# Moving wavelet and normalisation work between VectorE, GpSimd and ScalarE, and taking the quantiser's range from row extremes of h

## The reference

```python
# 1. wavelet tokeniser: three Haar analysis levels, then per level
w = softmax(stack([h, v, d]).reshape(B, -1) @ Wd + bd)          # 3 weights per image and level
rec = idwt2(rec, h * w[:, 0], v * w[:, 1], d * w[:, 2])         # Haar synthesis
h = rec
# 2. h = h + mixer(layernorm(h)): projections, a softplus, a cumulative sum along the
#    rows of an image, two products with Wc and Wd, biases bc + bd
# 3. h = h + ffn(layernorm(h)), quantised:
scale = sigmoid(clip_x) * max(abs(xn)) / 127                    # xn = layernorm(h), one scale for all
xq    = clip(round(xn / scale), -128, 127) * scale
gate, up = xq @ quant(w_gate).T, xq @ quant(w_up).T             # 704 columns
out   = quant(silu(gate) * up) @ quant(w_down).T
layernorm(x) = (x - mean(x)) / sqrt(var(x) + 1e-5)              # over a row of 256
```

## Time and profile before

| | us |
|---|---|
| median of 3 runs | 154.51 (152.99 to 154.53) |
| the profiled execution | 153.44 |
| its span, first to last instruction | 151.7 |
| VectorE busy in the span | 130.2 (86%) |
| TensorE busy | 116.7 (77%) |
| ScalarE busy | 78.3 (52%) |
| GpSimd busy | 43.7 (29%) |

### The profile page before, as it was taken

One profiled execution on the slowest core, in us unless ns is written; L12 is line 12 of the kernel. 1 busy time (PEld: TensorE's weight loads), 2 busy tenths in 40 slices (PEclk: granted clock), 3 DMA queues, 4 the chain that ended last, 5 costly groups with the idle time before them and its releaser, 6 DMA issues.

```text
span 151.7 us, 1953 instructions
## 1 busy us (share of the span) xinstructions
PE 116.7 (77%) x655; PEld 78.7 (52%) x660; DVE 130.2 (86%) x257; ACT 78.3 (52%) x143; POOL 43.7 (29%) x58
## 2 busy tenths in 40 slices
PE   0659839997779972999999903968999998799710
PEld 0649737896355451864888803334545433475400
DVE  0799599963599999999999999859989898999991
ACT  4004107103296642076398079977999990794000
POOL 6631000000400099950000404000766570005720
PEclk9999955999758999599999995599999999999996
DMA  4999700000000000000000000000000000001176
GB/s 110 385 367 402 327 4 6 0 0 0 0 0 0 0 6 0 0 0 0 0 0 4 0 0 2 0 0 0 2 4 0 0 0 0 0 4 69 73 230 181
DMA packets 3035, 8.26 MB, mean 54 GB/s; under 512 B 466, under 2 KB 722, under 8 KB 2898
## 3 DMA queue, kind: packets, MB, share of 16 engines
q1 hardware_dynamic: 2738, 7.62, 14.1%
q10 hardware_dynamic: 288, 0.52, 0.9%
HBM read 6.05 MB, written 2.10 MB: 54 GB/s over the span
## 4 chain that ended last, share of the span: by engine, by line
DVE 51%; PE 21%; ACT 11%; issue 10%; DMA 3%; POOL 2%; ACTq 0%; DVEq 0%; POOLq 0%
PE bank L471 6%; PE bank L414 4%; PE bank L444 4%; DVE middle L1223 4%; DVE state_mem L1230 3%; DVE stats L987 3%; DVE wabs L1027 3%; DVE amax L1196 3%; DVE raw L1255 3%; PE bank L419 3%; DMA early<-in_x 3%; ACT early L773 3%; DVE early L1005 3%; ACT raw L874 3%; ACT state_mem L867 2%
## 5 line engine op out<-in xcount | busy, mean ns | idle before, releaser
L389 POOL TENSOR_TENSOR rstd<-var,minus_half 128x8 f32<-128x8 f32 x4 | 6.8, 1702 | 61.7 <-DVE var L993 61.7
L614 PE MATMUL bank<-state_mem,wqT 128*128 128x512 bf16 x78 | 18.2, 379 | 0.8 <-DVE state_mem L1186 0.6
L401 POOL TENSOR_TENSOR early<-raw,state_mem 128x512 f32<-128x512 f32 x10 | 13.0, 1298 | 18.3 <-ACT raw L874 18.3
L773 ACT ACTIVATE early<-h,nmr,rstd 128x256 f32<-128x256 f32 x25 | 12.8, 587 | 6.7 <-DVE nmr L998 6.7
L558 PE MATMUL bank<-mixer_w,early 128*128 128x256 f32 x64 | 16.0, 407 | 0.0
L867 ACT ACTIVATE state_mem<-bank,gscale 128x512 f32<-128x512 f32 x22 | 15.1, 752 | 1.2 <-PE bank L614 1.0
L627 PE MATMUL bank<-wqT,middle 128*128 128x256 bf16 (+1 forms) x96 | 12.8, 274 | 2.4 <-DVE middle L1223 2.4
L419 PE MATMUL bank<-restart,ident 128*128 128x512 bf16 x47 | 13.6, 440 | 1.2 <-DVE var L993 0.9
L558 PEld LDWEIGHTS bank<-mixer_w,early 128*128 128x128 f32 x64 | 12.9, 207 | 3.0 <-issue 1.1
L1196 DVE TENSOR_REDUCE amax<-early 128x1 f32<-128x1024 f32 x11 | 13.3, 1212 | 0.4 <-POOL early L401 0.3
L614 PEld LDWEIGHTS bank<-state_mem,wqT 128*128 128x128 bf16 x80 | 7.4, 98 | 10.0 <-DVE early L1204 1.1
(11 more groups left out here) (148 smaller groups left out, 244.8 us busy)
## 6 DMA issues: line engine op xcount, KB each, us to landing
out<-early SPq DMA_DIRECT2D x7, 256.0 KB, 2.8
early<-in_x SPq DMA_DIRECT2D x1, 1024.0 KB, 9.0
wT<-in_dot_weights SPq DMA_DIRECT2D x1, 784.0 KB, 7.0
raw<-in_gate_rows SPq DMA_DIRECT2D x1, 768.0 KB, 10.6
raw<-in_up_rows SPq DMA_DIRECT2D x1, 768.0 KB, 11.9
raw<-in_down_rows SPq DMA_DIRECT2D x1, 768.0 KB, 13.2
early<-in_x ACTq DMA_DIRECT2D x2, 256.0 KB, 4.9
early<-in_x SPq DMA_DIRECT2D x2, 256.0 KB, 4.7
```

Of the source, the lines that this page charges most:

```text
L401: nc.gpsimd.tensor_tensor(act[:, u, :], up_s[:, m % UPS, :], silu[:, u % SIL, :], ALU.mult).then_inc(pool_act_ready, 1)
L614: last = nc.tensor.matmul(dst[:, :], w, xqT[:, k, c, :], start=(c == 0), stop=(c == CH - 1))
L773: nc.scalar.activation(xn[:, half, r, :], h[:, half, r, :], ACT.Identity, bias=nmr[:, norm, half, r:r + 1], scale=rstd[:, norm, half, r:r ...
```

## The change

Five things change.

1. Half 1's wavelet analysis goes to GpSimd (`analyse_second`), except the sums across columns and the two low bands of level 0, which VectorE keeps (`across_second`, `low_second`). TensorE's `haar_level` and ScalarE's copies of it go.
2. In the last synthesis level of both halves ScalarE scales the band D too, and GpSimd forms the two sums of V and D (`high_columns`).
3. The power -0.5 becomes Ln and Exp on ScalarE (`inverse_std`), right behind the moments; ScalarE normalises all rows; `add_bias` goes pair by pair.
4. The largest |xn| comes from the largest and the smallest element of each row of `h` (`extremes`, `reach_from_mean`), times the row's inverse deviation.
5. 32 of the 36 weight transposes stand ahead of most of half 1's mixing on TensorE, and their copies on ScalarE ahead of the second normalisation. `WARM_FFN` goes from 14 to 10. `weight_maxima(0)` moves to the wavelet stage, `coefficients` behind `xn_out(0)`.

```diff
+            def analyse_second():
+                add = nc.gpsimd.tensor_tensor
+                pool.wait_ge(x_in[-1], 16)
+                src = xt[:, 1, :, :]
+                seq.link(add(lohi1[0][:, 1, :, :], src[:, :, 0::2], src[:, :, 1::2], ALU.subtract))
+                for op, b in ((ALU.add, V_), (ALU.subtract, D_)):
+                    add(dst[:, b, :, :], lohi1[0][:, 1, 0::2, :], lohi1[0][:, 1, 1::2, :], op).then_inc(high_bands, 1)
+                pool.wait_ge(low_bands, 1)
+                for n in (1, 2):
...
+            def high_columns(half):
+                pool.wait_ge(v_ready, 4 * half + 4)
+                for odd, op in enumerate((ALU.add, ALU.subtract)):
+                    nc.gpsimd.tensor_tensor(syn[0][:, 1, odd::2, :], v, d, op).then_inc(high_ready, 1)
...
+            def inverse_std(norm, half):
+                sc.wait_ge(stats_ready, norm * HALVES + half + 1)
+                seq.link(nc.scalar.activation(var[...], stats[:, norm, half, :, 2], ACT.Ln, bias=eps[:, :], scale=1.0 / C))
+                nc.scalar.activation(rstd[...], var[...], ACT.Exp, scale=-0.5).then_inc(rstd_ready, 1)
...
             softplus(0)
             decay_rate(0)
-            normalise(0, 1, range(ACT_ROWS[1]))
+            inverse_std(0, 1)
+            normalise(0, 1, range(R))
...
+            def extremes(half, n):
+                nc.vector.tensor_reduce(hmax[:, half, rows], h[:, half, rows, :], AX.X, ALU.max)
+                return seq.mark(nc.vector.tensor_reduce(hmin[:, half, rows], h[:, half, rows, :], AX.X, ALU.min))
...
+            for n in range(R // 2):
+                step = extremes(0, n)
+            reach_from_mean(0, step)
             centre(1, 0)
-            step = add_mix(1, (1, 2, 3))
-            variances(1, 1, step)
-            dve.wait_ge(xn_ready, sum(ACT_ROWS) + R)
-            maximum(0, 0, slice(0, R)).then_inc(xmax_ready, 1)
+            for n in range(R // 2):
+                add_mix(1, (n,))
+                step = extremes(1, n)
+            seq.wait(reach_from_mean(1, step))
             centre(1, 1)
-            normalise_rows(1, 1, range(LAST_ACT_ROWS, R))
...
-            normalise(1, 1, range(LAST_ACT_ROWS))
-            ffn_weights_out(range(3, 5))
+            inverse_std(1, 1)
+            ffn_weights_out(range(4, 5))
+            normalise(1, 1, range(R))
             nc.scalar.preload_act_table_set("silu_and_others")
...
+            sc.wait_ge(xn_ready, 3 * R)
             nc.scalar.activation(xq_i[:, 0, TPB:R, :], ...)
```

More of the change, by code:

```diff
@@ L139, in build_tower @@
         acol = sb("acol", [P, 5])
+        lohi1 = [state_mem.take([P, 2, R >> n, C >> (n + 1)]) for n in range(3)]
+        state_mem.clear()
         za = state_mem.take([P, HALVES, PAIR])
@@ L224, in build_tower @@
         dve_seq, act_seq = sem("dve_seq"), sem("act_seq")
-        bands = [sem(f"bands{n}") for n in range(HALVES)]
-        minus_ready, haar_psum, haar_out = sem("minus_ready"), sem("haar_psum"), sem("haar_out")
+        bands = sem("bands")
+        low_bands, high_bands, coarse_bands = sem("low_bands"), sem("high_bands"), sem("coarse_bands")
         bT_psum = [sem(f"bT_psum{n}") for n in range(HALVES)]
@@ L455, in bands_transposed @@
                     piece = pieces[n]
[L456 to L460 removed]
+                    if half == 0:
+                        if n in (0, 12, 15):
+                            pe.wait_ge(bands, {0: 1, 12: 2, 15: 3}[n])
+                    elif n == 0:
+                        pe.wait_ge(low_bands, 2)
+                    elif n in (4, 8):
+                        pe.wait_ge(high_bands, n // 4)
+                    elif n in (12, 15):
+                        pe.wait_ge(coarse_bands, {12: 4, 15: 8}[n])
                     last = transpose(own(half, n // 4)[:, (n % 4) * P:(n % 4 + 1) * P], piece, ident[:, :])
@@ L493, in logits, with ffn_weights_transposed @@
                 nc.tensor.matmul(lz, ones[0:1, :], bias10[:, :], start=False, stop=True).then_inc(logits_done, 1)
-            def ffn_weights_transposed():
-                for n in range(36):
+            def ffn_weights_transposed(first, end):
+                for n in range(first, end):
                     kind, t, c = n // 12, n // 2 % 6, n % 2
@@ L999, in centre @@
                     ALU.mult, ALU.mult).then_inc(nmr_ready, 1)
-            def normalise_rows(norm, half, rows):
-                dve.wait_ge(nmr_ready, norm * HALVES + half + 1)
-                for r in rows:
-                    ts(xn[:, half, r, :], h[:, half, r, :], rstd[:, norm, half, r:r + 1], nmr[:, norm, half, r:r + 1], ALU.mult,
-                       ALU.add).then_inc(xn_late_ready, 1)
             def small_coefficients():
@@ L1126, in _ @@
             for n in range(R // 2):
-                step = moments(0, 1, n)
-            variances(0, 1, step)
+                moments(0, 1, n)
             small_coefficients()
@@ L1176, in quantise_input @@
                 rows = slice(g * TPB, (g + 1) * TPB)
+                dve.wait_ge(xn_ready, 2 * R + half * R + rows.stop)
                 if k == 1:
```

215 lines of the change are left out of this document (99 added, 116 removed).

## The result

The changed kernel takes **164.70 us**, median of 4 runs (163.76 to 165.59); the kernel before takes 153.96 beside it (4 runs, 152.99 to 154.53). The ratio is 1.067, 95% interval 1.060 to 1.074. The profiled execution took 164.58 us, 11.1 us more than before, with a span of 162.7. VectorE is busy 137.0 us of it (before 130.2), ScalarE 83.8 (78.3), GpSimd 51.1 (43.7), TensorE 117.3 (116.7). Every engine has more busy time, TensorE too, although its products of the Haar levels are gone.

What follows compares the result with a forecast made beforehand. VectorE was taken to bound the kernel. 153.44 us (profiled execution before) + 3.5 + 5.3 + 1.7 + 1.0 = 164.9; the forecast said 164.5, 160 to 169 for its own case, with a wider range of 156 to 169.

Steps and rivals of the forecast that it cites:

- The first term: Start of `step_size(1)` on VectorE, at 76.8 instead of 73.31 us: +3.5 us.
- the last two: `gate_up(0)` later behind `xtop` by 1.7 us, and the FFN starting at TensorE's lower clock, 1.0 us.
- Part 1: Half 1's analysis on GpSimd: VectorE held some 5.1 us by taking turns, half 0's synthesis 3.9 us late.
- Part 2: Last synthesis level: half 0's `nmr` about as before, half 1's columns of `h` at 52.7, 4.7 us late.
- Part 3: Half 1's normalisation: ScalarE's last row 4.9 us late, so `softplus(1)` ends at 76.8 and `step_size(1)` starts 3.5 late.
- Part 4: Extremes on VectorE, clamps to `xtop`: sixteen reductions at 0.69 us, 17.85 us in all instead of 12.5, +5.3.
- Part 5: ScalarE behind `xtop`: eight rows, table load and rounding in sequence; `gate_up(0)` 6.8 us after `xtop` instead of 5.1, +1.7.
- The FFN's clock: TensorE nearly idle before the FFN, which then starts at 1.2 GHz: 0 to 1.9 us lost, taken as 1.0.
- Analysis spared: Rival: taking turns matters little for the analysis; half 0's synthesis starts at 22.7, kernel 159 us; chance 0.12.
- not slower: Rival: nothing takes turns in the wavelet stage; `step_size(1)` 6.8 us early, kernel 153.6 to 154.6 us; chance 0.10.
- Cheap reductions: Rival: reductions at half price, -4.9 us; 149 us together with not slower (chance 0.05), 160 with the main forecast.
- TensorE's order: Rival: half 1's bank 3 ready later than 14 us after the clamps, bounding the kernel; 166 to 168 us; chance 0.05.

Runs made afterwards that it cites:

- analysis_held: The change, with GpSimd's analysis of half 1 waiting until VectorE has written half 1's two low bands: 162.98 us, 1.058 of the kernel before.
- std_before_rate: The change, with ScalarE's Ln and Exp of half 1 ahead of `decay_rate(0)`: 164.25 us, 1.064 of the kernel before.
- only_extremes: The kernel before plus row extremes, all half 1 rows normalised by ScalarE and 10 idle products: 163.71 us, ratio 1.065.
- early_table: The change, with ScalarE's table load ahead of half 1's eight rows instead of behind them: 163.09 us, 1.055 of the kernel before.
- old_pe: The change with TensorE's old order, all 36 weight transposes behind the mixer; extremes kept: 165.09 us, 1.073 of the kernel before.
- no_extremes: The change with the row extremes undone but TensorE's new order kept: 163.38 us, 1.064 of the kernel before.
- no_extremes_old_pe: The change with the row extremes and TensorE's new order undone, 10 idle products kept: 156.81 us, 1.021 of the kernel before.
- analysis_only: The change with `high_columns`, the row extremes and TensorE's new order undone, 10 idle products kept: 153.72 us, 0.999 of the kernel before.
- bias_held: The kernel before, with GpSimd's eight bias additions held back until VectorE runs instructions with at most one SBUF operand: 147.84 us, ratio 0.958.

## Why the prediction was right, point by point

The forecast was 164.5 us, from 160 to 169; 164.70 was measured. The sum in the forecast is 164.9, and no reason is given for the 0.4 taken off it. The first term came out 1.3 too high, the last two 0.3 and 0.5 too low, so that the sum is closer than its parts. The change in the time of the execution by its stages, in us, from the profiles of before and after:

| step | predicted | measured | from |
|---|---|---|---|
| `step_size(1)`, and with it the clamps | +3.5 | +2.2 | clamps 85.55 to 87.79 (`step_size(1)` +2.4, 73.31 to 75.71) |
| clamps to `xtop` | +5.3 | +5.2 | 12.5 to 17.69 |
| `xtop` to first product | +1.7 | +2.0 | 5.1 to 7.05 |
| FFN's start at 1.2 GHz | +1.0 | +1.5 | 9.43 late at its first product, 10.96 at `atop` |
| sum | +11.5 | +10.9 | the whole: 164.58 - 153.44 = 11.1 |

**Part 1 held in kind.** The synthesis of half 0 starts 2.7 late, not 3.9, because VectorE is held by some 3.8 us and not by 5.1: GpSimd's 1024 elements take 1.96 us and not my estimate of 2.35, and its sum and difference of 256 run mostly beside a reduction, which takes its usual 1.75. `own_strips(0)` came at 22.19, not 23.9; from there to the synthesis it took 3.9, not 3.4. (Of GpSimd's nineteen new instructions fifteen are this analysis and two belong to half 0.) VectorE's instructions beside GpSimd last longer, as said. `analysis_held` shows that it is the overlap, and not the work, that costs: the same instructions 4.8 us later give 3.1 us back at the synthesis.

**Part 2 failed in one step.** The synthesis of half 0 took 7.5 us up to the columns, not 6.6, which used up most of the 1.2 us by which part 1 was better. I put the columns of half 1 at 52.7 and they came at 52.20, but for another reason: I had VectorE waiting there for GpSimd's last sum. That sum ended at 50.89, the row at 52.20 names no releaser, and VectorE itself was last. Five of its instructions from 44.29 on last 7.2 us together; where GpSimd is idle such instructions take 0.35, 0.35, 0.42, 0.42 and 0.74, 2.3 us. So three bias additions and two sums on GpSimd held VectorE by 5 us, where I had counted only how they delay each other on GpSimd. That the size came out nearly right is luck: GpSimd's last sum ended 1.8 us ahead of my 52.7, and VectorE's own work, held for 5 us that I had not counted, ended at 52.10.

**Part 3 was mis-sized.** `step_size(1)` was predicted at 76.8, +3.5, and came at 75.71, +2.4. Everything ahead of it is early by the same: `step_size(0)` 57.86 (58.6), the rows' end 64.56 (65.3), `softplus(1)` 75.67 (76.8). Some 0.7 of the 1.1 stems from parts 1 and 2, and 0.4 from a shorter chain behind the last row. What failed is the size of the hold in part 1 and of this chain. `std_before_rate` corrects the reason as well: an earlier end of ScalarE's rows moves nothing, since TensorE's products ahead of `projections(1)` run at 1.2 GHz and bound it.

**Part 4 was right** to 0.2 us: sixteen reductions at 0.67 to 0.68, 0.58 to 0.60 apart, and `only_extremes` finds the same 17.6 us in the kernel before. What I did not see is that part 4 with its rows on ScalarE and its 10 idle products is worth 10.0 us by itself: 5.1 for the reductions, 2.0 for the rows, the load and the rounding behind `xtop`, and 2.7 for a slow clock behind those.

**Part 5.** ScalarE has no gap from `nmr` through the load to the rounding. The load lasts 1.28 us and the rounding starts 1.30 after it began: no drain shows, and `early_table` has 1.29 between load and first row. The step is 2.0 and not 1.7 mainly because `nmr` comes 0.28 us ahead of `xtop`, where I had 0.5. Had I gone by the Trainium skill ("ScalarE: Activation LUTs", "What ACT_TABLE_LOAD costs"), my estimate for the step would have been 3.1, where 2.0 was measured. The transposes took 3.57 us instead of 1.96 at 1.2 GHz, and bank 3 was ready 11.4 us behind the clamps and was asked for after 13.8, covered by 2.4 (predicted 12, 14, 2). `old_pe` confirms the cover. `no_extremes` shows how thin it was: a gain of more than those 2.4 us on VectorE would have stopped at TensorE.

**The FFN's clock came, but its reason isn't shown.** I put the 1.0 down to the time in which TensorE stands nearly idle, and called the four fewer idle products free. In `no_extremes_old_pe` and `analysis_only` the gap ahead of the first product is 0.56 and 0.59 us, as in the kernel before (0.56), and the FFN starts at the lower clock all the same. Nine of the ten kernels with 10 idle products start it so and lose 1.5 to 2.7 us in the FFN; the kernel before and the three others with 14 lose nothing (one profiled execution of each). So the fewer idle products, which also begin earlier, may be what costs here. A kernel that differs in them alone wasn't run, so this stays open. They are not without effect in any case: in `no_extremes_old_pe` and `analysis_only` the first product comes 3.8 us behind `xtop`, in the kernel before 5.1.

**The rivals.** *Analysis spared* needed a synthesis at 22.7 and *not slower* needed VectorE's lengths beside GpSimd to be those alone; the rows at 11.58 and 44.29 refute both, and `bias_held` shows the hold from the other side. *Cheap reductions* is refuted by 0.68 for 512. *TensorE's order* was not the bound in the change (covered by 2.4 us), but is the bound in `no_extremes`, at 163.4.

One term hid another throughout: 2.2 + 5.2 + 2.0 + 1.5 is the sum along the path, but single parts give 10.0 (part 4), 2.7 (part 2), 6.6 (TensorE's order uncovered), 0 (parts 1 and 3), which add to far more than 11. The 10.0 and the 0 have the 10 idle products and a slow start of the FFN in them.

## What to carry to other kernels

Work moved from VectorE to GpSimd is not off VectorE while both read from memory: price it by the length of VectorE's instructions beside GpSimd in the trace, and then place GpSimd's instructions beside VectorE's waits, reductions and reads of PSUM. Here eight additions placed so were worth 4.2%. And a maximum taken from row extremes reads everything twice on the critical engine; what stood beside the maximum (rows, table load) then stands behind it. Idle products that keep TensorE busy belong to what is varied alone: a change of their number may cost or hide as much as the change under test.
